# Attention phase of a one-core block: column-quartered logits, a spread choice of experts, two row buffers, the norm on VectorE, maxima split before their transpose, and another letter order

## What is computed

```python
x = x + cross_attention(layernorm(x), ctx)              # not touched
x = layernorm(x)
scores = einsum('bhqd,bhkd->bhqk', q, k) / sqrt(32)     # 16 heads of 32, 4 key heads, 2048 keys
attn = softmax(scores); out = einsum('bhqk,bhkd->bhqd', attn, v) @ ow + ob
src = rmsnorm(x + out, norm1_w)
logits = src @ gate_w                                   # 8 experts
probs = sigmoid(logits); _, sel = top_k(probs, 2); w_topk = probs[sel] / (sum + 1e-6)
ranks = cumulative count of each expert in row order - 1
valid = ranks < 1280                                    # capacity; a row past it is dropped
padded[sel * 1280 + ranks] = src                        # rows are scattered to the experts
h = gelu(einsum('ecd,edf->ecf', padded, w1)); out = einsum('ecf,efd->ecd', h, w2)
src + sum over the two choices of w_topk * out[slot], rmsnorm
```

## Time and profile before

| | us |
|---|---|
| median of 3 runs (lowest to highest) | 3563.71 (3556.47 to 3568.64) |
| the profiled execution | 3558.09 |
| its span | 3556.2 |
| busy in the span: PE / DVE / ACT / POOL | 3164.5 / 2184.4 / 1615.2 / 2012.8 |
| PE busy in chunks 1 to 6 (653.8 to 2129.1 us) | 1443.33 of 1475.30 |
| the 2048 maxima of L1132 on DVE | 1282.0 |
| the 2048 exponentials of L1052 on ACT | 1065.5 |
| the 352 adds of L920 and L924 on POOL | 1613.5 (586.8 + 1026.7) |

### The profile page before, as it was taken

One profiled execution on the slowest core, in us unless ns is written; L12 is line 12 of the kernel. 1 busy time (PEld: TensorE's weight loads), 2 busy tenths in 40 slices (PEclk: granted clock), 3 DMA queues, 4 the chain that ended last, 5 costly groups with the idle time before them and its releaser, 6 DMA issues. The chain is left out here.

```text
span 3556.2 us, 47058 instructions
## 1 busy us (share of the span) xinstructions
PE 3164.5 (89%) x16936; PEld 2047.9 (58%) x16936; DVE 2184.4 (61%) x3738; ACT 1615.2 (45%) x3252; POOL 2012.8 (57%) x912
## 2 busy tenths in 40 slices
PE   5877799999999999999999999975999999999900
PEld 4665444554454554544544545434999999999900
DVE  5776788778687778777787877712333333333245
ACT  2332166656555556555565655543334433333311
POOL 2342099879889889889798898871000000000064
PEclk7998599999999999999999999986999999999955
DMA  3443634222222213121121211003222222222066
GB/s 103 154 161 138 167 103 135 59 42 52 49 44 51 49 34 78 22 60 51 31 60 41 54 43 34 13 27 141 72 72 90 78 87 71 94 88 72 27 242 212
DMA packets 199217, 284.62 MB, mean 80 GB/s; under 512 B 86295, under 2 KB 91415, under 8 KB 196485
## 3 DMA queue, kind: packets, MB, share of 16 engines
q1 hardware_dynamic: 176720, 221.11, 21.8%
q0 software_dynamic: 16640, 51.77, 4.0%
q10 hardware_dynamic: 5685, 9.49, 0.7%
HBM read 169.17 MB, written 115.41 MB: 80 GB/s over the span
## 5 line engine op out<-in xcount | busy, mean ns | idle before, releaser
L1132 DVE TENSOR_REDUCE p_mxp<-p_ps_a 128x1 f32<-128x512 f32 x2048 | 1282.0, 681 | 251.7 <-PE p_ps_a L1308 238.5
L1052 ACT ACTIVATE p_PR<-p_ps_b 128x512 f32<-128x512 f32 x2048 | 1065.5, 603 | 787.0 <-PE p_ps_b L1322 773.4
L924 POOL TENSOR_TENSOR p_PP<-p_PP,p_PR 128x2048 f32<-128x2048 f32 x224 | 1026.7, 4583 | 37.8 <-ACT p_PR L1052 14.8
L1308 PE MATMUL p_ps_a<-p_KS,p_QS 96*128 96x512 f32 x2048 | 837.7, 441 | 33.9 <-DMA p_KS<-kh_d 17.0
L1322 PE MATMUL p_ps_b<-p_QS,p_KS 98*128 98x512 f32 x2048 | 761.7, 419 | 6.8 <-ACT p_PR L1052 5.9
L920 POOL TENSOR_TENSOR p_PP<-p_PR 128x2048 f32<-128x2048 f32 x128 | 586.8, 4584 | 214.6 <-ACT p_PR L1052 190.2
L1308 PEld LDWEIGHTS p_ps_a<-p_KS,p_QS 96*128 96x128 f32 x2048 | 391.0, 195 | 476.8 <-DVE p_mxp L1132 311.5
L1561 POOL DMA_DIRECT2D ye_d<-p_YE x80 | 43.3, 541 | 897.8 <-DVE p_YE L1670 897.8
L1328 PE MATMUL p_ps_pv<-p_PR,p_VS 128*32 128x512 f32 x4096 | 525.3, 614 | 0.0
L1322 PEld LDWEIGHTS p_ps_b<-p_QS,p_KS 98*128 98x128 f32 x2048 | 391.8, 192 | 204.6 <-ACT p_PR L1052 119.2
L1606 ACT ACTIVATE p_hf<-p_ps_h 128x384 f32<-128x384 f32 (+1 forms) x256 | 112.0, 438 | 558.6 <-PE p_ps_h L83 553.1
(11 more groups left out here) (169 smaller groups left out, 3398.1 us busy)
## 6 DMA issues: line engine op xcount, KB each, us to landing
p_w_raw<-in_L_ffn_w SPq DMA_DIRECT2D x16, 2048.0 KB, 8.6
...
```

Source lines behind the costliest of these rows:

```text
L924: nc.gpsimd.tensor_tensor(PP[:, buf, :, :], PP[:, buf, :, :], PR[:, tile_at(u, tile), :, :], ALU.add).then_inc(add_made, 1)
L1052: nc.scalar.activation(PR[:, tile_at(u, kt), j, :], ps_b[:, n % BK, :], ACT.Exp, scale=SCALE).then_inc(ex_made, 1)
L1132: nc.vector.reduce_max(mxp[:, a // (S // CH), a % (S // CH):a % (S // CH) + 1], ps_a[:, bank, :], AXX).then_inc(a_read, 1)
L1308: nc.tensor.matmul(ps_a[:, bank, :], QS[0:96, g, j, t * P:(t + 1) * P], KS[0:96, g, kb * CH:(kb + 1) * CH], start=True, stop=True).then_in ...
```

## The change

1. **Letters.** BASE is another order (the counts of A, B, V, D, M in a unit stay 64, 64, 16, 5, 1); four V of a unit are late instead of three; 15 A are early instead of 13. The A of the 16 kt were 3, 5, 4, 4, 4, 3, 3, 4, 4, 4, 5, 4, 4, 5, 4, 4 and are 2, 5, 5, 5, 4, 3, 4, 2, 2, 6, 2, 6, 3, 5, 6, 4; V and D stand in 13 runs of neighbours instead of 15. M keeps its place near the end of kt14: kt14, kt15 and the next kt0 began and ran "ABBABABAVVVM", "BABBAABAD", "VABBABAB" and are "BBAABABAVVVAMA", "BBBAABADA", "BBABAB", so that no V stands any longer ahead of the next unit's first B.
2. **Maxima.** The negation and the split are made on mxv itself (two instructions of 128x4x4, L1134 and L1136 of the kernel after, p_mhl) before the transpose; M transposes 8 rows instead of 4, one copy (L1143, p_mrow) brings them to SBUF, and the DMAs wait for that copy.
3. **Logits.** L is four matmuls with gate weights stationary (32 columns of the array each, one per quarter of the 512 features) and the 512 rows moving; VectorE copies the four partial results (p_lgq, L1185), and a new letter N in (g2, kt1) adds them in four small matmuls with a constant `fold`.
4. **Choice.** Spread over kt1 to kt4 of g2 instead of one place; `topf` and both one-hot rows are now in SBUF, where before `topf` and the first were in PSUM.
5. **Rows.** SR has two buffers; four of the eight sends stay in g3 (behind every second kt), four go to g0 of the next chunk.
6. **Norm.** The product with the norm's weights leaves GpSimd and the one with the root leaves ScalarE; VectorE does both in one instruction (`scale`, SR, root and norm_row, all in SBUF), one at each of kt6 to kt9 of g1.
7. Small: INVERT_1_AT 3 to 4, EXP_AT 1 to 2.

```diff
...
-    BASE = ["VABBABAB", "AVABAABBAB", "AVABABBAB", "VABBBAABA", "DABBABAAB", "ABBAVVBAB", "BAABBABV", "VAABABBAB",
...
-    EXTRA = {0: {11: "O", 13: "O", 15: "O"}, 1: {1: "O", 10: "R", 11: "R", 12: "R", 13: "R"}, 2: {0: "L", 8: "K"}, 3: {}}
...
+    BASE = ["BBABAB", "ABABABVABA", "ABAVABABAB", "ABABAVVBABA", "BABADABBA", "ABBABABVV", "BABABABA", "BABBABVVV",
...
+    EXTRA = {0: {11: "O", 13: "O", 15: "O"}, 1: {1: "O", 10: "R", 11: "R", 12: "R", 13: "R"}, 2: {0: "L", 1: "N", 8: "K"}, 3: {}}
     ORDER = [[BASE[kt] + EXTRA[g].get(kt, "") for kt in range(KT)] for g in range(KV)]
-    TURN, V_LATE, D_LATE = 13, 3, 1
+    TURN, V_LATE, D_LATE = 13, 4, 1
...
-    POWER_AT, NORM_AT, SCALE_AT = (1, 2), {(1, 1): (0, 1), (1, 3): (2, 3)}, {(1, 8): (0, 1), (1, 9): (2, 3)}
+    POWER_AT, SCALE_AT = (1, 2), {(1, 6): 0, (1, 7): 1, (1, 8): 2, (1, 9): 3}
 
     WEIGH_AT, RANK_AT, FINISH_AT = (2, 2), (2, 5), (2, 8)
-    EXP_AT, INVERT_1_AT, INVERT_2_AT, SUM_AT = 1, 3, 7, 12
-    SENDS = {(3, 0): (0,), (3, 1): (1,), (3, 2): (2,), (3, 4): (3,), (3, 5): (4,), (3, 6): (5,), (3, 7): (6,), (3, 9): (7,)}
+    TOP_AT, INDEX_AT, EXP_AT, HOT_AT, INVERT_1_AT, SELECT_AT, INVERT_2_AT, SUM_AT = 1, 2, 2, 3, 4, 4, 7, 12
+    SENDS = {(3, 1): 0, (3, 3): 1, (3, 5): 2, (3, 7): 3}
+    LATE_SENDS = {(0, 1): 4, (0, 3): 5, (0, 5): 6, (0, 7): 7}
...
-        SR = s.sb("SR", [P, TT, D])
+        SR = s.sb("SR", [P, 2, TT, D])
...
-            def load_y(c, first):
-
-                if first:
+            def load_y(c):
+
+                if c == 0:
                     sp.wait_ge(zero_st, 16 * NZ)
-                else:
-                    sp.wait_ge(sent, 16 * 2 * TT * c)
+                elif c >= 2:
+                    sp.wait_ge(sent, 16 * 2 * TT * (c - 1))
                     gate(sp)
-                    sp.wait_ge(src_st, 16 * c)
+                    sp.wait_ge(src_st, 16 * (c - 1))
                 gate(sp)
-                sp.dma_start(SR[:], y_d[bass.ds(c, 1)].rearrange("a (t p) d -> p (a t) d", p=P)).then_inc(y_in, 16)
-
-            def maxima_to(g, n):
-
-                hold(ml_made, n)
-                sp.dma_start(f32(QS[96:97, g, :, :]), f32(mh[:])).then_inc(m_in, 16)
-                sp.dma_start(f32(QS[97:98, g, :, :]), f32(ml[:])).then_inc(m_in, 16)
+                sp.dma_start(SR[:, c % 2], y_d[bass.ds(c, 1)].rearrange("a (t p) d -> p (a t) d", p=P)).then_inc(y_in, 16)
+
+            def maxima_to(g, read):
+
+                hold(a_read, read)
+                sp.dma_start(f32(QS[96:97, g, :, :]), f32(mrow[0:G, :])).then_inc(m_in, 16)
+                sp.dma_start(f32(QS[97:98, g, :, :]), f32(mrow[G:2 * G, :])).then_inc(m_in, 16)
...
-            def norm(c, t):
-
-                pool.wait_ge(ss_made, TT * c + t + 1)
-                nc.gpsimd.tensor_tensor(SR[:, t, :], SR[:, t, :], norm_row[:], ALU.mult).then_inc(normed, 1)
...
+                            send(c - 1, (SENDS[g, n],))
+                        if (g, n) in LATE_SENDS and c > 1:
+                            send(c - 2, (LATE_SENDS[g, n],))
...
-            def scale(c, t):
-                act.wait_ge(rstd_made, c + 1)
-                act.wait_ge(normed, TT * c + t + 1)
-                nc.scalar.activation(SR[:, t, :], SR[:, t, :], ACT.Copy, scale=sr_rstd[:, t:t + 1]).then_inc(sr_made, 1)
...
+                    dve.wait_ge(mxv_made, u + 1)
+                    nc.vector.tensor_scalar(mhl[:, :, 0, :], mxv[:], -1.0, None, ALU.mult).then_inc(mh_made, 1)
+                    dve.wait_ge(mh_made, u + 1)
+                    nc.vector.scalar_tensor_tensor(mhl[:, :, 1, :], mxv[:], -1.0, f32(mhl[:, :, 0, :]), ALU.mult, ALU.subtract).then_inc(ml_made, 1)
 
             def maxima_split(u, at, first=False):
                 count, bank = at
                 dve.wait_ge(a_mm, count + 1)
                 if not first:
                     dve.wait_ge(m_in, 32 * u)
-                nc.vector.tensor_scalar(mh[:], ps_a[0:G, bank, :], -1.0, None, ALU.mult).then_inc(mh_made, 1)
-                dve.wait_ge(mh_made, u + 1)
-                nc.vector.scalar_tensor_tensor(ml[:], ps_a[0:G, bank, :], -1.0, f32(mh[:]), ALU.mult, ALU.subtract).then_inc(ml_made, 1)
-                dve.wait_ge(ml_made, u + 1)
-                dve.sem_inc(a_read, 1)
+                nc.vector.tensor_copy(mrow[:], ps_a[0:2 * G, bank, :]).then_inc(a_read, 1)
...
+            def scale(c, t):
+                dve.wait_ge(rstd_made, c + 1)
+                nc.vector.scalar_tensor_tensor(SR[:, c % 2, t, :], SR[:, c % 2, t, :], sr_rstd[:, t:t + 1], norm_row[:],
+                                               ALU.mult, ALU.mult).then_inc(sr_made, 1)
...
-            def choose(c, at):
-
+            def quarters_out(c, at):
+                count, bank = at
+                dve.wait_ge(a_mm, count + 1)
+                nc.vector.tensor_copy(lgq[:], ps_a[:, bank, :]).then_inc(a_read, 1)
+
+            def logits_out(c, at):
                 count, bank = at
                 dve.wait_ge(a_mm, count + 1)
                 if c > 0:
                     dve.wait_ge(placed, PLACED * c)
-                nc.vector.tensor_scalar(lgt[:], ps_a[:, bank, 0:TT * E].rearrange("p (t e) -> p t e", t=TT), 17.5, None, ALU.min).then_inc(lgt_made, 1)
-                dve.wait_ge(lgt_made, c + 1)
+                nc.vector.tensor_scalar(lgt[:], ps_a[:, bank, 0:TT * E].rearrange("p (t e) -> p t e", t=TT), 17.5, None, ALU.min).then_inc(a_read, 1)
+
+            def top_two(c, read):
+                dve.wait_ge(a_read, read)
                 gate(dve)
                 for t in range(TT):
                     nc.vector.max(top[:, t, :], lgt[:, t, :]).then_inc(route, 1)
+
+            def top_indices(c):
                 dve.wait_ge(route, ROUTES * c + TT)
                 gate(dve)
                 for t in range(TT):
                     nc.vector.max_index(topi[:, t, :], top[:, t, :], lgt[:, t, :]).then_inc(route, 1)
+
+            def one_hot(c):
                 dve.wait_ge(route, ROUTES * c + 2 * TT)
-
-                topf = ps_a[:, bank, TT * E:TT * E + 2 * TT].rearrange("p (t k) -> p t k", t=TT)
-                first = ps_a[:, bank, 2 * TT * E:3 * TT * E].rearrange("p (t e) -> p t e", t=TT)
-                nc.vector.tensor_copy(topf, topi[:, :, 0:2]).then_inc(route, 1)
+                nc.vector.tensor_copy(topf[:], topi[:, :, 0:2]).then_inc(route, 1)
                 dve.wait_ge(route, ROUTES * c + 2 * TT + 1)
-                nc.vector.tensor_tensor(first, topf[:, :, 0:1].broadcast_to((P, TT, E)), per_expert(iota_e[:]), ALU.is_equal).then_inc(route, 1)
-                nc.vector.tensor_tensor(oh[:, 1, :, :], topf[:, :, 1:2].broadcast_to((P, TT, E)), per_expert(iota_e[:]), ALU.is_equal).then_inc(route, 1)
-                dve.wait_ge(route, ROUTES * c + 2 * TT + 3)
-                nc.vector.tensor_tensor(sel[:], first, oh[:, 1, :, :], ALU.add).then_inc(sel_made, 1)
-                nc.vector.tensor_copy(oh[:, 0, :, :], first).then_inc(a_read, 1)
+                for k in range(2):
+                    nc.vector.tensor_tensor(oh[:, k, :, :], topf[:, :, k:k + 1].broadcast_to((P, TT, E)), per_expert(iota_e[:]), ALU.is_equal).then_inc(route, 1)
+
+            def select(c):
+                dve.wait_ge(route, ROUTES * (c + 1))
+                nc.vector.tensor_tensor(sel[:], oh[:, 0, :, :], oh[:, 1, :, :], ALU.add).then_inc(sel_made, 1)
...
-                pe.wait_ge(mxv_made, u + 1)
-                for t in range(TT):
-                    last = nc.tensor.transpose(ps_a[0:G, bank, t * P:(t + 1) * P], mxv[:, t, :], ident[:])
+                pe.wait_ge(ml_made, u + 1)
+                for t in range(TT):
+                    last = nc.tensor.transpose(ps_a[0:2 * G, bank, t * P:(t + 1) * P], f32(mhl[:, t, :, :]).rearrange("p m j -> p (m j)"), ident[:])
...
-                for t in range(TT):
-                    for k in range(DK):
-                        last = nc.tensor.matmul(ps_a[:, bank, t * E:(t + 1) * E], srT[:, t, k, :], gw[:, k, :], start=(k == 0), stop=(k == DK - 1))
+                for k in range(DK):
+                    last = nc.tensor.matmul(ps_a[32 * k:32 * (k + 1), bank, :], gw[:, k, :], srT[:, :, k, :], start=True, stop=True)
+                last.then_inc(a_mm, 1)
+
+            def logits_summed(c, at, quarters_read):
+                bank = take(at)
+                pe.wait_ge(a_read, quarters_read)
+                for t in range(TT):
+                    last = nc.tensor.matmul(ps_a[:, bank, t * E:(t + 1) * E], lgq[:, t * P:(t + 1) * P], fold[:], start=True, stop=True)
...
```

More of the change, by code:

```diff
@@ L668, in phase_attend @@
     SCALE = float(HD) ** -0.5
-    ROUTES, PLACED = 11, 18
+    ROUTES, PLACED = 2 * TT + 3, 18
     ZR = 4
@@ L701, in slots @@
                 for pos, what in enumerate(ORDER[g][kt]):
-                    if what in "ORLK" and first or what == "M" and last and g == KV - 1 or what in "BVD":
+                    if what in "ORLNK" and first or what == "M" and last and g == KV - 1 or what in "BVD":
```

(25 more changed lines are left out.)

77 lines of the change are left out of this document (44 added, 33 removed).

## The result

The changed kernel takes 3640.64 us (median of 4, 3632.11 to 3646.75), the kernel before 3560.09 (median of the 4 runs beside it). The ratio is 1.0222, 95% interval 1.0188 to 1.0256: slower by 80.6, and the whole interval lies above 1. The forecast was 3619, slower, range 3480 to 3700. The profiled execution took 3646.75; its span is 3645.1, 88.9 more than in the earlier trace rows.

The account below looks back on a forecast made before the run. PE's own sequence was taken to bound a unit, POOL 4.7 us behind. Letters -3, logits and POOL chain -56 and -10, tail -2.5 and +.5 gave 3487; VectorE against POOL, +132, made it 3619, range 3480 to 3700.

Parts of the forecast that it names:

- the likeliest case: DVE's SBUF instructions wait for POOL's running add, those following within .03 us sharing a turn: 3619, range 3570 to 3680, chance .58.
- Rival B: DVE's SBUF instructions beside POOL's adds: no conflict that PE feels; 3487, up to 3550 with half covered; chance .25.
- rival C: Maxima split: the second instruction also misses POOL's gap and waits, 4.6 each in 17 of 32 units; 3725; chance .14.
- The sum without the port: Whole kernel, all terms but DVE's conflict with POOL: -71, giving 3487.
- L and the sends: g2 and g3: L falls from 3.63 to 1.2 and its clock loss (3.4) goes; three sends fewer before POOL's add, 1.15 each.
- The -56 for chunks 1 to 6: g2 and g3: PE needs 112.5 against 121.9, -9.4 a chunk, with POOL's chain of about 110 just under it.
- Letters and maxima: Every unit's letter order and early maxima split: gains and charges sum to -.1 a unit, -3 us in 32.
- The stall of .3 for the maxima's DMA: First B of a unit: the DMA needs 3.9 to 4.0 after M, letters between take 3.8 or less, +.3.
- The port's price: DVE's SBUF instructions at scale, choice and split waiting for POOL's adds: +132 in all.
- choice: g2: the second one-hot waits a whole add; 4.0 lost and 1.7 clock, 5.7 x 7 = +40.
- Scale: g1: four instructions wait for adds; PE loses 6.8 and about 1 of clock, 7.8 x 7 = +55.
- Split: Once in each of 31 units: the first waits 2.2, the second .3, with 1.2 covered; +37.

Follow-up runs that it names:

- e1: The changed kernel with norm and root, choice and maxima split put back as in the kernel before; 3519.11 us, ratio .9885.
- e8: The kernel before with DVE probes of eight kinds behind kt2, kt6 and kt12 of each unit; 3725.22 us, read only for its instructions.
- e4: The changed kernel with norm and root back, the maxima's high part a second reduction, low part, one-hot and select on POOL; 3481.00 us, ratio .9781.
- e12: e2 with L as 16 matmuls of 8 columns as before and without N; 3535.54 us.
- e11: e2 with all eight sends in g3 as before; 3531.62 us.
- e2: e1 with the order strings and V_LATE = 3 of the kernel before; 3497.09 us, ratio .9820.
- e9: e4 with BASE and V_LATE of the kernel before; 3494.69 us.
- e3: The changed kernel with the choice's two one-hot instructions merged into one; 3600.23 us.
- e7: The changed kernel with the choice in one place and in PSUM as before, behind N; 3609.14 us.
- e5: The changed kernel with the maxima split after the transpose as before, on PSUM; 3578.37 us.

## Why the prediction was right

**The place and the sign.** That the change would lose to the port was the likeliest case and happened at all three places. The trace agrees with the mechanism to the instruction: the cast takes .62 where its own time is .17, so it waits .45 (forecast .9), one one-hot passes, the other takes 4.53 where its own time is .19 (nearly a whole add), the second splitting instruction never waits. Rival B (no conflict that PE feels, .25) is refuted by e1 and e8, rival C (both splitting instructions miss) by L1136's 32 times .17. The Trainium skill's "SBUF — State Buffer", in its section on who interferes with whom, lists copies and scalar operations among those that can compete with GpSimd and says that a reduction never does. e8 agrees, with the copy and the scalar operation at 1.9 to 2.1 us and the reduction at .21; no run here looked into the reciprocal's reason.

**The sum without the port** was 3487; e4 gives 3481, with the norm and root where they were before. Its g2 + g3 take 57.3 + 55.1 = 112.4, forecast 112.5. The two terms in it, L and the sends, are worth 38 and 35 by e12 and e11, each undone alone; both together are worth 61 (e2 against before), not 73, since a wait in g3 comes back when either is undone. The -56 for chunks 1 to 6 stood, as e2's chunks 1 to 6 show (1423.8 against 1475.3, -51.5). Where the earlier add comes from was wrongly explained (see e12).

**Letters and maxima**, -3: the balance holds (a bare unit takes 55.0 in e4 and before), its items do not. The early split, in e4's form, gives .7 a unit (55.7 in e1, 55.0 in e4) with the new letters and 1.0 (55.0 in e2, 54.0 in e9) with the old, more than the .4 that is left of my -.7 and +.3; the letters take .7 (e1 against e2) to 1.0 (e4 against e9) where I had -.6 and +.9. The stall of .3 for the maxima's DMA came in two of 31 units only (.64 and .82): elsewhere the first B comes 4.1 after M (1314.25 to 1318.38 in the kernel after) and does not wait.

**The port's price**, +132, measured 160 between e4 and the change. The step that was off is the clock. I charged 1 us of it at scale and 1.7 at the choice, and none at the split. The trace has .50 beside or just behind 25 of the 35 stops over 1 us in chunks 0 to 6. The window behind scale's second stop and the one behind the choice:

```profile
1284.50:1294.80 10.30, 9.73 (x33) 5.21 (x29) 9.80 (x12) 4.91 (x9) 2.42 (x1) 0.50 0.00 0
1339.20:1346.00 6.80, 6.13 (x20) 3.03 (x24) 6.04 (x12) 2.28 (x4) 1.85 (x3) 0.50 1.01 229
```

These cost some 4.9 and 3.1, half of PE's busy time in them; the one behind scale is 3.4 us long in some chunks and 10.2 in others. In e1, e2 and e4, whose longest stop in chunks 1 to 6 is .98, there is no such stretch. By terms: *choice* 40 was forecast; e3 took off 40 and e7 32. *Scale* was put too high: four instructions take 8.6 and not 10.4 us, since the first met an add near its end (1.7), and PE stops 3.3 and not 6.8; between e5 and e1 g1 falls by 4.0 a chunk, not 7.8. *Split* was put too low: PE stops .3, 1.1, 1.7 and 3.2 in g0 to g3, on the mean 1.6 and not 1.2, 1.5 in chunk 0, and the clock falls behind; e5 took off 62 even with the late split's own cost in it. By the recorded terms (2.2 and .3 less 1.2) the split makes 1.3 a unit and 40, not 37. Half an add as the mean wait was near (L1134 takes 1.95 on the mean, .17 of it its own), but the order of the letters fixes the phase, so each place has its own value, nearly the same in all chunks. POOL is busy for 89% of chunks 1 to 6, not 95% as the prediction has it. That the total came within 22 us is in part luck: scale's 55 was twice what the trace gives it (28, by e5 against e1), and the split's 37 little over half of the 62 that e5 took off.
